# Gate stage of a gated cross-attention block on Trainium2: second half of x3 made by ScalarE and GpSimd, reciprocal roots moved to VectorE

## The reference

```
x3 = x2 + tanh(g_xattn[1]) * (yn * gn_w + gn_b + ctx)        # per batch, channel = token row
n  = (x3 - mean(x3)) / sqrt(var(x3) + 1e-5)                  # over the 512 numbers of a token
logits = n @ gate_w.T + gate_b;  e = argmax(softmax(logits))
out = x3 + tanh(g_ffn[1]) * (n @ expert_w[e].T + expert_b[e])
```

## Time and profile before

| | us |
|---|---|
| median of 3 runs | 770.32 |
| lowest, highest | 770.23, 770.71 |
| profiled execution, its own time | 771.58 |
| its span in the trace | 769.8 |

### The profile page before, as it was taken

The page is one execution under the profiler, slowest core; times in us unless marked ns, Lnnn a source line. Parts: engine busy times, 40 slices in busy tenths (PEclk is TensorE's granted clock), DMA queues, the critical chain, the costliest instruction groups (busy, mean ns, idle before and its releaser), DMA issues.

```text
span 769.8 us, 12438 instructions
## 1 busy us (share of the span) xinstructions
PE 746.3 (97%) x3875; PEld 588.6 (76%) x3875; DVE 458.0 (59%) x1017; ACT 429.0 (56%) x1274; POOL 277.2 (36%) x436
## 2 busy tenths in 40 slices
PE   8999999999999999999999999999999999987997
PEld 7888887788788887878778788887887753565875
DVE  4796403556656466555655555655548777887643
ACT  3753326565556556555655656555655557756731
POOL 0531006244244325324423523523322457714333
PEclk9999999999999999999999999999999999997999
DMA  8545461401232040140231104203133054835142
GB/s 310 183 145 182 137 190 57 188 19 69 62 139 76 14 179 29 69 178 14 69 150 55 68 21 173 74 23 125 30 132 109 1 177 162 330 153 194 44 120 72
DMA packets 40654, 87.04 MB, mean 113 GB/s; under 512 B 5497, under 2 KB 25465, under 8 KB 36626
## 3 DMA queue, kind: packets, MB, share of 16 engines
q1 hardware_dynamic: 37540, 78.45, 28.8%
q0 software_dynamic: 3056, 7.89, 3.0%
HBM read 70.02 MB, written 35.05 MB: 136 GB/s over the span
## 4 chain that ended last, share of the span: by engine, by line
PE 87%; DVE 6%; ACT 2%; issue 2%; POOL 2%; DMA 1%; POOLq 0%; SPq 0%; DVEq 0%; ACTq 0%
PE banks L970 8%; PE banks L972 7%; PE banks L1004 7%; PE banks L971 7%; PE banks L1006 7%; PE banks L1005 7%; PE banks L954 7%; PE banks L991 3%; PE banks L436 3%; PE banks L434 3%; PE banks L435 3%; PE banks L983 2%; PE banks L1962 2%; PE banks L1963 2%; PE banks L1964 2%
## 5 line engine op out<-in xcount | busy, mean ns | idle before, releaser
L638 ACT ACTIVATE p_sb<-p_sb,nmax 128x128 f32<-128x128 f32 x256 | 99.7, 391 | 56.6 <-DVE nmax L858 56.5
L633 ACT ACTIVATE oT_hi<-banks 128x512 fp32r<-128x512 f32 x64 | 38.2, 596 | 132.7 <-PE banks L1017 132.6
L895 DVE SCALAR_TENSOR_TENSOR x_sb<-banks,tgates,x_sb 128x512 f32<-128x512 f32 x64 | 47.9, 749 | 63.1 <-PE banks L1006 63.1
L750 POOL TENSOR_TENSOR v_lo<-v_raw,v_hi 128x128 fp32r<-128x128 f32 x64 | 29.5, 461 | 125.3 <-ACT v_hi L681 125.3
L853 DVE SCALAR_TENSOR_TENSOR p_sb<-banks,q_rstd,mask 128x128 f32<-128x128 f32 x256 | 71.4, 340 | 2.5 <-POOL q_rstd L89 2.4
L755 POOL TENSOR_TENSOR p_sb<-p_sb,rsum 128x512 f32<-128x512 f32 x64 | 66.6, 1041 | 15.1 <-DVE rsum L885 15.1
L954 PEld LDWEIGHTS banks<-kT,qT_sb 128*128 128x128 f32 x512 | 66.9, 191 | 5.4
L954 PE MATMUL banks<-kT,qT_sb 128*128 128x128 f32 x512 | 67.3, 274 | 0.0
L842 DVE TENSOR_TENSOR oT_lo<-banks,oT_hi 128x512 fp32r<-128x512 f32 x64 | 44.0, 688 | 31.9 <-ACT oT_hi L633 31.8
L885 DVE RECIPROCAL rsum<-prob_sum 128x4 f32<-128x4 f32 x64 | 11.3, 176 | 80.7 <-ACT p_sb L638 80.7
L889 DVE TENSOR_TENSOR pT_lo<-banks,pT_hi 128x512 fp32r<-128x512 f32 x64 | 44.1, 690 | 23.1 <-ACT pT_hi L656 23.1
(11 more groups left out here) (297 smaller groups left out, 1897.5 us busy)
## 6 DMA issues: line engine op xcount, KB each, us to landing
sorted_x<-in_empty SPq DMA_DIRECT2D x8, 2064.0 KB, 10.9
w_raw<-in_wq_l SPq DMA_DIRECT2D x8, 1024.0 KB, 5.9
w_raw<-in_wo_l SPq DMA_DIRECT2D x8, 1024.0 KB, 4.8
exp_w<-in_exp_w_l SPq DMA_DIRECT2D x8, 1024.0 KB, 8.8
kT_scr<-kT_st SPq DMA_DIRECT2D x16, 256.0 KB, 2.4
v_scr<-v_st SPq DMA_DIRECT2D x16, 256.0 KB, 2.5
xs<-sorted_x SPq DMA_DIRECT2D x15, 258.0 KB, 2.7
v_raw<-v_scr SPq DMA_DIRECT2D x14, 256.0 KB, 2.6
```

The costliest lines, as they stand in the source:

```text
L638: last = act.activation(p_sb[:, b % 2, h * P:(h + 1) * P], p_sb[:, b % 2, h * P:(h + 1) * P], ACT.Exp, bias=nmax[:, b % 2, h:h + 1], accum ...
L895: dve.scalar_tensor_tensor(out=s.x[:, b, :], in0=o_ps[b % 2][:, :], scalar=s.tgates[:, 0:1], in1=s.x[:, b, :], op0=ALU.mult, op1=ALU.add). ...
```

## The change

x3 of batches 4 to 7 is no longer made by `update` on VectorE. ScalarE multiplies z by `a_col` in place (`scale_z`), GpSimd adds `ctx_res` into `xrow` (`add_z`). The roots of both halves, `rstd(c)`, move from GpSimd to VectorE. On VectorE the four updates stand in a row ahead of all statistics, and root, shift, choice and position of the first half stand ahead of the later statistics. On ScalarE `copy_gateT(0)` goes ahead of `seed(0)`, `copy_gateT(1)` ahead of `seed(1)`. On TensorE the narrow products behind transposes 4 to 7 go, `logits(0)` moves one transpose ahead, `gates(1)` behind `ranks(0)`, and two wide products, 512 columns each, stand between `logits(1)` and `ranks(1)`. The semaphore of x3 is one for each half.

```diff
@@ scalar @@
             act.wait_ge(s.res_done, B)
-            for b in range(HB):
-                copy_x3T(b)
+            act.wait_ge(s.centred, B)
+            act.wait_ge(s.a_done, 1)
+
+            def scale_z(b):
+                act.activation(s.z[:, b, :], s.z[:, b, :], ACT.Identity, scale=s.a_col[:, b:b + 1]).then_inc(z_scaled, 1)
+
+            scale_z(4)
+            scale_z(5)
+            copy_x3T(0)
+            scale_z(6)
+            copy_x3T(1)
+            copy_x3T(2)
+            copy_x3T(3)
+            scale_z(7)
+            copy_gateT(0)
             seed(0)
-            copy_gateT(0)
             for b in range(HB, B):
                 copy_x3T(b)
+            copy_gateT(1)
             seed(1)
-            copy_gateT(1)
@@ gpsimd @@
-            def rstd(c):
...
+            def add_z(b):
+                pool.wait_ge(z_scaled, b - HB + 1)
+                pool.tensor_tensor(xrow[:, b, 0:D], s.z[:, b, :], s.ctx_res[:, b, :], ALU.add).then_inc(x3_done[1], 1)
...
-            rstd(0)
-            rstd(1)
+            pool.wait_ge(s.res_done, B)
+            for b in range(HB, B):
+                add_z(b)
             pool.wait_ge(s.filled, 16 * E)
             pool.wait_ge(s.token_set, 2)
             scatter(0)
@@ vector @@
+            def rstd(c):
+                cols = slice(c * HB, (c + 1) * HB)
+                dve.wait_ge(xseed_done, c + 1)
+                dve.wait_ge(xval_done, c + 1)
+                newton_rsqrt(dve, newton, 3 * c, xval[:, cols], xseed[:, cols], xtmp[:, cols], xrow[:, cols, RSTD],
+                             s.c15).then_inc(xrstd_done, 1)
...
-            update(0)
-            update(1)
+            for b in range(HB):
+                update(b)
             stats(0)
-            update(2)
             stats(1)
             aggregate(0)
-            update(3)
             stats(2)
             aggregate(1)
             stats(3)
             aggregate(2)
             aggregate(3)
             half_var(0)
-            update(4)
-            update(5)
             stats(4)
-            update(6)
             aggregate(4)
-            stats(5)
-            update(7)
-            aggregate(5)
-            stats(6)
+            rstd(0)
             shift(0)
             choose(0)
+            stats(5)
+            aggregate(5)
+            position(0)
+            stats(6)
+            stats(7)
             aggregate(6)
-            stats(7)
             aggregate(7)
             half_var(1)
-            position(0)
+            rstd(1)
             shift(1)
             choose(1)
             position(1)
@@ tensor @@
                 last.then_inc(x3T_done, 1)
-                keep_warm(2)
+                if b < HB:
+                    keep_warm(2)
...
             gates(0)
             transpose_x3(4)
+            logits(0)
             transpose_x3(5)
-            logits(0)
             transpose_x3(6)
             transpose_x3(7)
-            gates(1)
...
             ranks(0)
+            gates(1)
             logits(1)
+            for _ in range(2):
+                pe.matmul(x3T_ps[0][:, :], s.ident[:, :], s.g[:, 0, :], start=True, stop=True)
             ranks(1)
```

More of the change, by code:

```diff
@@ L1561, in experts @@
         xs, xn, xsT_hi, xsT_lo = s.xs, s.xn, s.xsT_hi, s.xsT_lo
-        x3_done, bn_done, mv_done = m.sem("x3_done"), m.sem("bn4_done"), m.sem("mv4_done")
+        x3_done, bn_done, mv_done = [m.sem(f"x3_done{c}") for c in range(2)], m.sem("bn4_done"), m.sem("mv4_done")
+        z_scaled = m.sem("z_scaled")
         gateT_done, gateT_copied = m.sem("gateT_done"), m.sem("gateT_copied")
@@ L1714, in update @@
                 dve.scalar_tensor_tensor(out=xrow[:, b, 0:D], in0=s.z[:, b, :], scalar=s.a_col[:, b:b + 1],
-                                         in1=s.ctx_res[:, b, :], op0=ALU.mult, op1=ALU.add).then_inc(x3_done, 1)
+                                         in1=s.ctx_res[:, b, :], op0=ALU.mult, op1=ALU.add).then_inc(x3_done[0], 1)
             def stats(b):
-                dve.wait_ge(x3_done, b + 1)
+                dve.wait_ge(x3_done[b // HB], b % HB + 1)
                 dve.bn_stats(s.bn[:, b, :], xrow[:, b, 0:D]).then_inc(bn_done, 1)
@@ L1870, in transpose_x3 @@
             def transpose_x3(b):
-                pe.wait_ge(x3_done, b + 1)
+                pe.wait_ge(x3_done[b // HB], b % HB + 1)
                 reached(pe, x3T_copied, b - 3)
```

## The result

| | before | changed |
|---|---|---|
| median of 20 runs each, us | 770.87 | 771.57 |
| lowest | 769.85 | 770.28 |
| ratio, 95% interval | | 1.0015 (1.0008 to 1.0022) |
| profiled execution, us | 771.58 | 773.51 |

The ratio says that the change makes the kernel slower by 0.15%, and its interval leaves out 1; the medians differ by 0.70 us, the means by 1.07. The range held the median, but the forecast of no change did not come true.

A forecast was written before the change was run, and what follows sets the result against it. The prediction took the gate stage's chain to the start of the list, set by the end of ranks(1), as the bound. Choice(1) +1.1 and ranks(1) -1.0 summed to about 0: 770.3 us, range 768.7 to 772.2.

The forecast's parts named there:

- forecast of no change: Whole kernel: later choice(1) and shorter ranks(1) cancel, giving 770.3 us; chance 0.40.
- The shared access: Gate stage: VectorE updates with two SBUF inputs wait for GpSimd's running adds, +1.07 us each for updates 2 and 3, +2.1 together.
- half_var(0) was to wait 0.4: VectorE, gate stage: this small SBUF operation meets GpSimd's last add and waits 0 to +0.4 us, taken as +0.4.
- rival (1): Gate stage: GpSimd stands aside or the two do not meet; choice(1) -0.1 us, or -0.6; total 769.2 or 768.7; chance 0.27.
- +1.1: VectorE, gate stage: choice(1) starts at 693.7 against 692.64, 1.1 us later.
- -1.0: TensorE: ten records of ranks(1) take about 1.36 us at the full clock, saving 1.0 us if the clock stays.
- the one of TensorE: Ahead of ranks(1): wide products take 1.98 us, end at 694.8, cost nothing; ranks(1) then gains 1.0 us if the clock stays.
- rival (2): TensorE: clock falls before the two wide products, delaying ranks(1); +1.3 to +2.3 us, so 771.6 to 772.6; chance 0.18.

The follow-up runs named there:

- e2: The changed kernel with GpSimd's adds made to wait for VectorE's fourth update; ratio to before 1.0006 (0.9997 to 1.0014).
- e4: The changed kernel with one narrow product behind each of transposes 4 to 7 and three ahead of logits(1); ratio to before 0.9995 (0.9986 to 1.0003).
- e9: The same kernel as e4, repeated on another chip; ratio to before 1.0001 (0.9992 to 1.0010).
- e8: The changed kernel measured once more, with nothing altered; ratio to before 1.0006 (0.9998 to 1.0015).
- e1: The changed kernel without the two wide products ahead of ranks(1); ratio to before 1.0020 (1.0011 to 1.0029).
- e10: The changed kernel with GpSimd's adds behind the fourth update and without the two wide products; ratio to before 0.9999 (0.9991 to 1.0008).
- e11: The changed kernel with only three narrow products added ahead of logits(1), none behind transposes 4 to 7; ratio to before 0.9998 (0.9989 to 1.0006).
- e5: The changed kernel with adds behind the fourth update, one narrow product behind each of transposes 4 to 7, three ahead of logits(1); ratio to before 0.9987.
- e7: The changed kernel with all eight updates on VectorE again, new order and roots on VectorE kept; ratio to before 1.0049 (1.0037 to 1.0061).

## Why the prediction was wrong

**Where it held.** The shared access was taken as a wait for two-input operations, which no row had shown. Updates 2 and 3 were to lose 1.07 us each; they took 1.78 and 1.76 us instead of 0.75, a loss of 1.03 and 1.01. Choice(1) was put 16.2 us after `a_col`, measured 16.18; half_var(0) was to wait 0.4, it took 0.56 instead of 0.17. With late adds, rival (1)'s -0.1 came out as -0.05 (e2). The Trainium skill (SBUF — State Buffer, section "SBUF: two separate sides") states this wait as an exclusive lock held for a whole instruction. The traces agree for this pair of operations: 1.76 to 1.78 us beside an add, 0.75 with the adds moved away (e2). Ranks(1) at the full clock was put at 1.36 us, measured 1.30 (e4). The forecast's sum, +1.1 and -1.0, is what e4 and e9 measure when the clock holds: ranks(1) ends at 19.09 and 19.07 against 19.04, and the first product comes at 34.68 and 34.48 against 34.61.

**The step that failed** is the one of TensorE: "at the full clock ... if the clock stays", with the wide products ending at 694.8 and costing nothing. I saw that the clock decides, gave the case in which it falls ahead of them 0.18, and took the forecast from the case in which it holds as if all executions were alike. They are not: by their times 8 of 20 fell there, and 6 of 12 in e8; one of each was profiled, and in both it had fallen ahead of logits(1). The evidence in the earlier trace rows was one execution, in which the clock had held until 16.3 us after `a_col`; I read it as a property of the kernel. Nothing of the changed kernel sets that moment alone: it came at 13.9, 13.7 (e8) and 14.2 us (e1), and at 12.3 with late adds (e2) and 14.2 with late adds and no wide products (e10), with TensorE's order the same up to there.

**Its price was also too low.** I gave +1.3 to +2.3. Profiled, the first product came 2.84 (and 2.48, e8) later than before. The 2.84 add up from choice(1) 1.07 later, 1.60 that ranks(1) waited for the wide products (3.19 us behind the start of choice(1) instead of 1.59), ranks(1) 0.16 shorter, and 0.33 behind it. Four wide records took 3.76, put at about 3.6, and logits(1), itself at the low clock, 1.87 instead of 1.06, which I had left out. From the list on (15.05 us to the first product, against 14.72) the 0.33 is the clock again: it came back at 708.12, and the 32 filling records behind `ew_lo` took 10.10 us instead of 9.72. Nor did all of it arrive at the end, as the prediction had it: from the first product to the end it is 57.15 us in the changed kernel, 57.66 before, and between 56.8 and 58.1 in all 13 profiles; with that and an `a_col` 0.40 sooner, 1.93 of the 2.84 are left in the profiled times.

What the groups make together: 12 runs at 771.06 and 8 at 773.50 against a mean before of 770.96 (and a median of 770.87). In time the lower group is the forecast (0.1 above before) and the upper one rival (2) (+2.5). For the upper one the two profiles show it; for the lower one it is argued, from its times and from e4 and e9. Its five runs at the clock of 0.991 or 0.992 had a longer time at the low clock somewhere, and where is not known. That the median moved is mostly the share of the upper group. That it stayed within the range is luck: it is the middle of a mixture that the sum did not have.

**Left open.** What makes the clock fall in one execution and hold in the next was not tried by itself; the runs only show that with the idle 0.72 us ahead of logits(1) filled, no upper group was seen in 33 runs of two kernels (e4, e9, e11), on chips where the changed kernel itself was not run, and in the 11 of e5 on a chip where it was. The wait of half_var(0) with late adds (1.14 us) was not taken away.

## What to carry to other kernels

Work placed ahead of a waiting operation to hold TensorE's clock is itself priced by the clock: four wide records took 1.96 or 3.76 us here. Fill the earlier gap first, with short products, and put the wide ones behind it. Before moving elementwise work to GpSimd, look at which VectorE operations with two SBUF inputs, or small ones on SBUF, run at that moment; a start after them (one more wait) brought choice(1) 1.1 us sooner here. Where times form two groups, forecast the share of each, and not the likelier one alone.

## What the runs showed of the hardware that was not expected

- VectorE's four-column half_var(1) took 0.44 us instead of 0.17 beside GpSimd's indirect transfer (691.25 to 692.29 in the profile of the changed kernel), and ended 0.03 us before it. All ten profiles in which the two meet have 0.44 or 0.45. It is not so for every small operation: three of the root's, beside the next transfer (692.59 to 693.55), took their 0.16 to 0.20. Why was not tried. It cost nearly nothing, since the second seed came at 692.35.
- With adds back to back from 2.9 to 7.9 us after `a_col` (e2), half_var(0) took 1.14 us and the first operation of the root 0.49: each ended 0.02 or 0.03 us behind the end of an add, half_var(0) with another add still to come. A small operation waits for the add that is running, not for all, so VectorE gets in between GpSimd's operations as GpSimd does between VectorE's.
- A fall of the clock also reached VectorE's side: in e7 logits(1) took 1.88 us and gates(1) 1.94, and choice(1) waited 0.55 for them.
